# Last stage of an adaLN transformer block with routed experts: normalised rows go through PSUM, in groups of 2, 4, 4, 4 and 2 batches of straight-line code

## The reference

```
out = scatter_add(expert rows * gate) + hidden_states         # acc_rows in DRAM
mu, var = mean(out), mean((out - mu)**2)                      # per token, 256 features
y = (out - mu) * rsqrt(var + 1e-5) * gamma + beta
x = x + gb * y                                                # gb: one row of 256 per batch
```

## Time and profile before

| what | value |
| --- | --- |
| time, median of 3 runs | 1625.9 us (1625.34 to 1626.49) |
| profiled execution, its own time | 1625.48 us |
| span of the profiled execution | 1623.7 us |
| last stage, from its first SP instruction to the end of the span | 1527.2 to 1623.7 us |
| busy in the whole span | PE 82%, DVE 71%, ACT 46%, POOL 34% |

### The profile page before, as it was taken

How to read it: one execution, slowest core, us unless ns; L and a number is a source line. 1 busy time by engine, 2 the same in 40 slices (tenths; PEclk the granted TensorE clock), 3 DMA queues, 4 the chain that set the end, 5 groups by cost and what they waited for, 6 DMA issues and landing times. The chain is left out here.

```text
span 1623.7 us, 24084 instructions
## 1 busy us (share of the span) xinstructions
PE 1327.1 (82%) x5919; PEld 937.7 (58%) x5920; DVE 1145.3 (71%) x2512; ACT 740.7 (46%) x1442; POOL 556.0 (34%) x928
## 2 busy tenths in 40 slices
PE   6499999999999999999999999999511595979200
PEld 3266666666666666666666666666411595868200
DVE  2368877778777787777877778777367744656387
ACT  1366656556565565655656556564200003333052
POOL 1101423234232342323423234223310356667247
PEclk7599999999999999999999999999855556989655
DMA  4000011010110101101011010110120103232464
GB/s 108 14 14 27 1 53 49 4 52 0 53 48 4 53 0 52 47 6 52 0 53 50 3 40 1 40 40 1 44 54 0 52 0 82 36 85 33 116 220 142
DMA packets 68360, 70.29 MB, mean 43 GB/s; under 512 B 13568, under 2 KB 64176, under 8 KB 68160
## 3 DMA queue, kind: packets, MB, share of 16 engines
q1 hardware_dynamic: 44272, 44.82, 9.2%
q10 hardware_dynamic: 18960, 18.88, 3.5%
q0 software_dynamic: 5056, 5.85, 2.3%
HBM read 40.35 MB, written 28.92 MB: 43 GB/s over the span
## 5 line engine op out<-in xcount | busy, mean ns | idle before, releaser
L830 PE MATMUL PS<-PF,V 128*128 128x512 f32 x1024 | 523.9, 593 | 0.0
L561 ACT ACTIVATE PF<-PS 128x512 f32<-128x512 f32 x512 | 303.0, 595 | 345.0 <-PE PS L756 343.4
L733 DVE TENSOR_REDUCE NMAX<-PS 128x1 f32<-128x512 f32 x512 | 346.5, 687 | 160.7 <-PE PS L765 150.5
L755 PE MATMUL PS<-Q,K 128*128 128x512 f32 x512 | 405.8, 792 | 0.9 <-ACT PF L561 0.9
L531 POOL TENSOR_TENSOR XL<-XF,XH 128x512 fp32r<-128x512 f32 x64 | 84.2, 1316 | 445.7 <-ACT XH L636 445.7
L765 PE MATMUL PS<-K,Q 128*128 128x512 f32 x512 | 203.6, 398 | 6.0 <-DVE NMAX L733 5.9
L756 PE MATMUL PS<-Q,K 128*128 128x512 f32 x512 | 202.7, 396 | 0.0
L830 PEld LDWEIGHTS PS<-PF,V 128*128 128x128 f32 x1024 | 174.5, 189 | 36.2 <-issue 6.7
L579 ACT ACTIVATE Q<-PS 64x512 fp32r<-64x512 f32 x256 | 151.5, 592 | 67.8 <-PE PS L93 63.0
L755 PEld LDWEIGHTS PS<-Q,K 128*128 128x128 f32 x512 | 97.2, 190 | 123.5 <-issue 105.4
L756 PEld LDWEIGHTS PS<-Q,K 128*128 128x128 f32 x512 | 97.4, 190 | 121.7 <-issue 121.6
(11 more groups left out here) (286 smaller groups left out, 2534.6 us busy)
## 6 DMA issues: line engine op xcount, KB each, us to landing
X<-in_L_attn_x SPq DMA_DIRECT2D x16, 512.0 KB, 5.0
MODB<-mod_rows SPq DMA_DIRECT2D x16, 512.0 KB, 4.4
h_rows<-H ACTq DMA_DIRECT2D x16, 512.0 KB, 3.1
acc_rows<-H ACTq DMA_DIRECT2D x16, 512.0 KB, 4.1
A<-acc_rows SPq DMA_DIRECT2D x16, 512.0 KB, 8.3
out_x<-X SPq DMA_DIRECT2D x16, 512.0 KB, 2.9
W1F<-in_L_ffn_W SPq DMA_DIRECT2D x3, 1024.0 KB, 4.9
W2F<-in_L_ffn_W SPq DMA_DIRECT2D x3, 1024.0 KB, 5.8
```

Source lines behind the costliest of these rows:

```text
L561: s_exp.done(act.activation(PF[:, u % 4, :], st_bank(u), ACT.Exp))
L733: s_mred.done(dve.tensor_reduce(NMAX[:, h % 2, c:c + 1], mx_bank(u), AX.X, ALU.max, negate=True))
L755: pe.matmul(st_bank(u), K1[:, kp, keys], Q1[:, h, :], start=True, stop=False)
L830: s_pv.done(pe.matmul(pv_bank(h), V1[:, vp, c, :], PF[:, u % 4, :], start=(c == 0), stop=(c == TC - 1)))
```

## The change

The load of GBG moves into `route`'s SP stream, between the load of B2 and the wait for the keys, and its tile is allocated ahead of `route`. `last_norm` is written anew, without loops. Batches go in groups of 2, 4, 4, 4 and 2. A pair is two chunks, 128x512, so there are 32 pairs. ACT writes its normalised chunks to PSUM, one bank per pair, eight banks in rotation; DVE multiplies a pair out of PSUM by GBG into A; POOL adds pair by pair. `bn_aggr` is gone: variance and mean are put together from the even and odd halves that `bn_stats` leaves, in steps 0 to 5. POOL computes the power -0.5 of the variance for a whole group (128x8 or 128x16), and one Newton step and the shift are DVE's steps 6 to 9.

The DVE's order is a list of phases. In phase j it does the statistics of group j, the ten steps of group j-1, and the products of group j-2, in slots of one chunk's statistics each: steps 0 to 5 in the first 3/8 of the slots, steps 6 to 9 in the last 5/16 (8 slots: first three and last three; 16 slots: first six and last five), and the products spread evenly. On POOL the power of group j stands ahead of the adds of group j-1.

```diff
+        m["GBG"], m["s_gbg"] = sb("GBG", [P, NB, D]), sem("tgbg")
...
             sp.dma_start(m["B2"][:, :, :], ap["L0_ffn_b2"].partition_broadcast(P)).then_inc(m["s_b"], 16)
+            sp.dma_start(m["GBG"][:, :, :], m["mod_dram"][:, 4, :].partition_broadcast(P)).then_inc(m["s_gbg"], 16)
             sp.wait_ge(s_key, TC)
...
+    GROUPS = (2, 4, 4, 4, 2)
+    FIRST = [sum(GROUPS[:j]) * TC for j in range(len(GROUPS) + 1)]
+    STEPS, VAR_DONE, PAIRS, BANKS = 10, 6, NCH // 2, 8
...
+            for b in range(NB):
+                sp.dma_start(batch(A, b), batch(acc_rows, b)).then_inc(s_in[b], 16)
+            for b in range(NB):
+                sp.wait_ge(s_add, 2 * b + 2)
+                sp.dma_start(batch(out_rows, b), batch(X1, b)).then_inc(s_out, 16)
...
+            def stats(c):
+                if c % TC == 0:
+                    dve.wait_ge(s_in[c // TC], 16)
+                    dve.memset(GATE[:, c // TC:c // TC + 1], 0.0).then_inc(s_gate, 1)
+                dve.bn_stats(S6[:, c, :], A[:, c, :]).then_inc(s_stat, 1)
+            def step(j, k):
+                if k == 0:
+                    dve.wait_ge(s_stat, FIRST[j + 1])
+                    dve.tensor_scalar(t, m2_e, 1.0 / D, EPS, ALU.mult, ALU.add).then_inc(s_step, 1)
+                elif k == 1:
+                    dve.tensor_tensor(d, mean_e, mean_o, ALU.subtract).then_inc(s_step, 1)
...
+                elif k == 6:
+                    dve.wait_ge(s_pow, j + 1)
+                    dve.tensor_tensor(t, y, y, ALU.mult).then_inc(s_step, 1)
...
+            def scale(q):
+                dve.wait_ge(s_xn, 2 * q + 2)
+                dve.tensor_tensor(A[:, 2 * q:2 * q + 2, :], pair_bank(q).rearrange("p (c n) -> p c n", c=2),
+                                  GBG[:, 2 * q // TC:2 * q // TC + 1, :].broadcast_to([P, 2, D]), ALU.mult).then_inc(s_mul, 1)
+            for j in range(len(GROUPS) + 2):
+                chunks = range(FIRST[j], FIRST[j + 1]) if j < len(GROUPS) else range(0)
+                chained = 1 <= j <= len(GROUPS)
+                pairs = range(FIRST[j - 2] // 2, FIRST[j - 1] // 2) if j >= 2 else range(0)
+                slots = max(len(chunks), 8 if chained else 0)
+                early, late = slots * 3 // 8, slots - slots * 11 // 16
+                for i in range(slots):
+                    if i < len(chunks):
+                        stats(chunks[i])
+                    if chained and i < early:
+                        for k in range(i * VAR_DONE // early, (i + 1) * VAR_DONE // early):
+                            step(j - 1, k)
+                    if chained and i >= slots - late:
+                        at, left = i - (slots - late), STEPS - VAR_DONE
+                        for k in range(at * left // late, (at + 1) * left // late):
+                            step(j - 1, VAR_DONE + k)
+                    for q in pairs[i * len(pairs) // slots:(i + 1) * len(pairs) // slots]:
+                        scale(q)
...
+                act.wait_ge(s_step, STEPS * (j + 1))
+                for c in range(FIRST[j], FIRST[j + 1]):
+                    if c % 2 == 0 and c // 2 >= BANKS:
+                        act.wait_ge(s_mul, c // 2 - BANKS + 1)
+                    act.activation(pair_bank(c // 2)[:, c % 2 * D:(c % 2 + 1) * D], A[:, c, :], ACT.Identity,
+                                   scale=Y[:, c:c + 1], bias=NMR[:, c:c + 1]).then_inc(s_xn, 1)
...
+            def power(j):
+                cols = slice(FIRST[j], FIRST[j + 1])
+                pool.wait_ge(s_step, STEPS * j + VAR_DONE)
+                pool.tensor_tensor(Y[:, cols], VAR[:, cols], HALF[:, cols], ALU.pow).then_inc(s_pow, 1)
+            power(0)
+            for q in range(PAIRS):
+                for j in range(1, len(GROUPS)):
+                    if 2 * q == FIRST[j - 1]:
+                        power(j)
+                pool.wait_ge(s_mul, q + 1)
+                x = X1[:, 2 * q:2 * q + 2, :]
+                pool.tensor_tensor(x, x, A[:, 2 * q:2 * q + 2, :], ALU.add).then_inc(s_add, 1)
```

More of the change, by code:

```diff
@@ L33 @@
 UNITS = H * TC
-RSQRT_SEED, RSQRT_OPS = 0x5F3759DF, 13
 class Stream:
@@ L93, in hi_lo_matmul @@
     return eng.matmul(out, lhs[1], rhs[0], start=False, stop=last)
[L96 to L108, removed]
 def build_program(nc, ap, out):
@@ L1429, in last_norm, with batch, pair_bank @@
 def last_norm(nc, out, m, sem, sb):
[L1432 to L1447, removed]
+    X1, PS, GBG, s_gbg = m["X1"], m["PS"], m["GBG"], m["s_gbg"]
+    GROUPS = (2, 4, 4, 4, 2)
+    FIRST = [sum(GROUPS[:j]) * TC for j in range(len(GROUPS) + 1)]
+    STEPS, VAR_DONE, PAIRS, BANKS = 10, 6, NCH // 2, 8
+    A = sb("A", [P, NCH, D])
+    S6 = sb("S6", [P, NCH, 6])
+    VAR, DEL, SUM, Y, TMP, NMR = (sb(x, [P, NCH]) for x in ("VAR", "DELt", "SUMt", "Yr", "TMP", "NMR"))
+    GATE, HALF = sb("GATEt", [P, NB]), sb("HALFt", [P, NCH])
+    s_half = sem("thalf")
+    s_in = [sem(f"tin{b}") for b in range(NB)]
+    s_pow, s_gate, s_stat, s_step, s_xn, s_mul, s_add, s_out = (sem(x) for x in ("tpow", "tgate", "tstat", "tstep", "txn", "tmul", "tadd", "tout"))
     acc_rows = m["acc_dram"][0:NT, :].rearrange("(c p) n -> p c n", p=P)
     out_rows = out.rearrange("b (c p) n -> p (b c) n", p=P)
-    def chunk(i, par, c):
-        return A[:, bass.ds((i * 2 + par) * GC + c, 1), :].rearrange("p c n -> p (c n)")
+    def batch(tile, b):
+        return tile[:, b * TC:(b + 1) * TC, :]
+    def pair_bank(q):
+        return PS[:, q % BANKS, :]
     with nc.Block() as block:
@@ L1473, in _ @@
         def _(dve):
[L1474 to L1510, removed]
@@ L1511, in _ @@
-            stats(GROUPS // 2 - 1, 1)
-            scale(GROUPS // 2 - 1, 0)
-            scale(GROUPS // 2 - 1, 1)
+            def stats(c):
[5 more added lines that the diff above has]
+                cols = slice(FIRST[j], FIRST[j + 1])
+                v, d, t, y, s, nmr = (x[:, cols] for x in (VAR, DEL, TMP, Y, SUM, NMR))
+                mean_e, m2_e, mean_o, m2_o = (S6[:, cols, i] for i in (1, 2, 4, 5))
+                if k == 0:
[3 more added lines that the diff above has]
+                    dve.tensor_tensor(d, mean_e, mean_o, ALU.subtract).then_inc(s_step, 1)
+                elif k == 2:
+                    dve.wait_ge(s_step, STEPS * j + 1)
+                    dve.scalar_tensor_tensor(out=v, in0=m2_o, scalar=1.0 / D, in1=t, op0=ALU.mult, op1=ALU.add).then_inc(s_step, 1)
+                elif k == 3:
+                    dve.wait_ge(s_step, STEPS * j + 3)
+                    dve.tensor_tensor(t, d, d, ALU.mult).then_inc(s_step, 1)
+                elif k == 4:
+                    dve.tensor_tensor(s, mean_e, mean_o, ALU.add).then_inc(s_step, 1)
+                elif k == 5:
+                    dve.wait_ge(s_step, STEPS * j + 4)
+                    dve.scalar_tensor_tensor(out=v, in0=t, scalar=0.25, in1=v, op0=ALU.mult, op1=ALU.add).then_inc(s_step, 1)
+                elif k == 6:
+                    dve.wait_ge(s_pow, j + 1)
+                    dve.tensor_tensor(t, y, y, ALU.mult).then_inc(s_step, 1)
+                elif k == 7:
+                    dve.wait_ge(s_step, STEPS * j + 7)
+                    dve.scalar_tensor_tensor(out=t, in0=t, scalar=-0.5, in1=v, op0=ALU.mult, op1=ALU.mult).then_inc(s_step, 1)
+                elif k == 8:
+                    dve.wait_ge(s_step, STEPS * j + 8)
+                    dve.scalar_tensor_tensor(out=y, in0=t, scalar=1.5, in1=y, op0=ALU.add, op1=ALU.mult).then_inc(s_step, 1)
+                elif k == 9:
+                    dve.wait_ge(s_step, STEPS * j + 9)
+                    dve.scalar_tensor_tensor(out=nmr, in0=s, scalar=-0.5, in1=y, op0=ALU.mult, op1=ALU.mult).then_inc(s_step, 1)
@@ new lines, in scale @@
+            def scale(q):
+                dve.wait_ge(s_xn, 2 * q + 2)
+                dve.tensor_tensor(A[:, 2 * q:2 * q + 2, :], pair_bank(q).rearrange("p (c n) -> p c n", c=2),
+                                  GBG[:, 2 * q // TC:2 * q // TC + 1, :].broadcast_to([P, 2, D]), ALU.mult).then_inc(s_mul, 1)
+            dve.wait_ge(s_gbg, 16)
+            for j in range(len(GROUPS) + 2):
[16 more added lines that the diff above has]
+                        scale(q)
+                if not slots:
+                    for q in pairs:
+                        scale(q)
@@ L1515, in _ @@
         @block.scalar
         def _(act):
[L1517 to L1525, removed]
+            for j in range(len(GROUPS)):
+                act.wait_ge(s_step, STEPS * (j + 1))
[4 more added lines that the diff above has]
+                                   scale=Y[:, c:c + 1], bias=NMR[:, c:c + 1]).then_inc(s_xn, 1)
@@ L1527, in _ @@
         @block.gpsimd
         def _(pool):
[L1529 to L1536, removed]
+            pool.memset(HALF[:, :], -0.5).then_inc(s_half, 1)
@@ new lines, in _ @@
+            pool.wait_ge(s_half, 1)
+            def power(j):
+                cols = slice(FIRST[j], FIRST[j + 1])
```

(2 more changed lines are left out.)

## The result

The changed kernel takes 1605.37 us (median of 4 runs, 1601.33 to 1606.51) against 1625.62 of before (4 runs, 1622.47 to 1626.49). The ratio is 0.9874, with a 95% interval of 0.9853 to 0.9896: 20 us less, where 19 were forecast.

A forecast was written before the change was run, and what follows sets the result against it. Bounds: the late GBG, and VectorE and GpSimd taking turns in products and adds. Five phases, twelve last adds to 1601.2 and 3.5 to the end gave span 1604.7, plus 1.8: 1606.5 us, 19 less; range 1598 to 1614.

The forecast's parts named there:

- The early load of GBG at nothing: In routing, the moved load of GBG was counted at nothing; without cover, 2 to 5 us at most.
- the 0.6: VectorE's small steps beside GpSimd's adds: each waits the remainder of the add in progress, 0.6 us on average.
- the 1.2: VectorE's small steps that need the one before: each waits a whole add, 1.2 us, as the next add slips in.
- The power: GpSimd's power in the last stage: 3.0 us on 16 columns and 1.7 on 8, nearer to a cost by column.
- The rival of the cheap power: GpSimd's power costs 1.0 us on 16 columns, a fixed cost; time 1602; chance 0.15.
- Adds of pairs 4 to 11: GpSimd in phase 3: eight adds of 1.23 plus 0.4 for four DVE steps let in, 10.2 us, to 1569.3.
- Twelve last adds: GpSimd after the last power: twelve adds in a row, 12 x 1.23 + 0.3 = 15.1 us, to 1601.2.
- to the end 3.5: From the last add's end through its store to the span's end: 3.5 us, as in the kernel before.
- Rival 3: VectorE's small steps do not wait for GpSimd's adds; time 1600.5; chance 0.13.
- rival 2: GpSimd's adds keep the turn, so a small step waits until scaled pairs run out; time 1613; chance 0.10.
- rival 4: The product out of PSUM still takes turns with adds: 28 x 0.61 = 17 us more, 1623.6; chance 0.03.
- rival 5: Slower than before: GpSimd's power becomes the bound, from some 9.5 us per 16 columns, time past 1629; chance 0.02.

The follow-up runs named there:

- Steps in PSUM: The changed kernel with TMP and SUM of the small steps in PSUM, seven banks left to the pairs: 1601.01 us, stage 72.1 against 76.0.
- the product out of SBUF: The changed kernel with ScalarE writing normalised chunks back to A in SBUF and VectorE multiplying from there: 1614.61 us, stage 84.7 against 76.0.
- the multiplication: The changed kernel with ALU.mult in place of ALU.pow on GpSimd, output not the reference's: 1601.25 us, stage 69.8 against 76.0.
- the two equal stages: 76.0 us for the changed kernel (1605.37) and 75.8 for the kernel before with GBG early and normalised rows through PSUM, old order kept (1604.05).

## Why the prediction was right

Its mechanism held: products and adds stopped taking turns, the early GBG cost nothing, and GpSimd's stream of powers and adds ended last. Its time was 1.1 us off, and that is closer than its parts, so in part luck. The span of the profiled execution was 5.2 us under the forecast: 3.7 of it is the earlier start of the stage, which nobody forecast, and 1.5 the stage. By its own steps, in us from the start of the stage (forecast, measured):

- First statistics 4.0, 4.1; step 9 of group 0 13.3, 13.2. The early load of GBG at nothing: right.
- Step 5 of groups 1, 2, 3 and 4: 16.7, 28.8, 43.5, 56.3 forecast; 16.3, 28.7, 42.8, 56.3 measured. These hold the guess that a small step waits out the add in progress. For the 0.6 a step among statistics and products waited 0.20 to 0.95 us beyond its 0.15, 0.55 on average of sixteen. For the 1.2 a step right behind another, or behind the power, waited 1.04 to 1.16. The reason given there was too narrow: step 1 needs nothing of step 0 and still lost the turn (1.15 and 1.16). Steps in PSUM showed the mechanism by taking it away.
- The power: 2.90 and 1.65 us measured for 3.0 and 1.7. From 4 to 8 to 16 columns (1.02, 1.65, 2.90) it is 0.39 plus 0.157 a column. The rival of the cheap power is out.
- Adds of pairs 4 to 11, forecast 10.2, and 12 to 19, forecast 10.5: 9.8 and 9.8. This is the term with the largest error of its own: I counted 0.1 for each step let in between adds, and they cost the adds nothing. In phase 5 step 5 then came after the adds, not before, and GpSimd waited 0.86.
- Twelve last adds 15.1, measured 14.7; to the end 3.5, measured 3.3.

The stage's 1.5 us less than forecast is these adds, the last run and 0.2 at the end. Rival 3 (steps don't wait) is excluded by the rows above, rival 2 (adds keep the turn) too, as no step took over 1.31 us; rival 4 by products of 662 to 692 ns; rival 5 by the power's size. Rival 4's price of 17 us was itself too high for this order: the product out of SBUF cost 8.7.

What the prediction did not see, since it did not ask, is that the new order is worth nothing over the old one once both have GBG early and the product out of PSUM. Without PSUM the new order is worth 5.9 (90.6 to 84.7), as it lowers how often products and adds meet. PSUM takes that away, and with it the order's use. The new order has costs that the old one has not, waits of small steps beside adds (3.9 us by the steps in PSUM) and the powers (6.2 by the multiplication). That they just cancel what it saves is argued from the two equal stages; its parts were not tried one by one.

## What to carry to other kernels

Where VectorE and GpSimd work side by side, look at the longest and shortest duration of one operation: a factor of two or three, as 3.36 against 1.22 us here, is a sign that they take turns. Letting VectorE read one of its operands from PSUM ended it here, for operations of 16 columns as for those of 1024. Before reordering a pipeline, make such a repair alone in the old order; here it and one earlier load gave the whole 20 us. An engine that waits on the path is not repaired by giving it other work first when the thing it waits for is part of a loop through another engine.

## What the runs showed of the hardware

- Step 0, a TENSOR_SCALAR with a single SBUF input, also waited for adds while it wrote to SBUF (153 to 1101 ns), and did not when it wrote to PSUM (156 to 171). I had counted it as free, so the prediction's wording, that one SBUF input does not exclude GpSimd, is too wide for it.
- A GpSimd add is not delayed by VectorE's small steps between: adds started 1.22 us apart with and without them, while the steps took up to 1.31 us, up to 1.16 of it waiting. A product of 0.68 with two SBUF inputs did delay adds (up to 1.80 us for 1.26).
- A power on GpSimd does not shut VectorE out as an add does: in the kernel with the product from SBUF, products of two SBUF inputs took 0.66 to 0.68 us in the middle of powers of 3.29 and 2.03, and up to 1.76 beside adds.
- ScalarE's 128x256 normalisation takes 551 ns on average into PSUM (the change) and 587 into SBUF (before, and the product from SBUF).
- The start of the last stage, after some 1525 us of work that is the same but for one load, moved by up to 6.8 us between profiles, with granted TensorE clocks of 0.883 to 0.891 over the span. What moves it was not tried.
